# Gated cross-attention with FFN: small GpSimd steps moved to VectorE, x staged by tile, the second batch's context turned in 32x32 blocks, all orders rewritten

## The reference

```python
xn = layernorm(x)
scores = (xn @ ctx.T) / 16            # (B, 256, 1601), masked columns -> -1e30
attn = softmax(scores)
x = x + tanh(g_xattn) * where(any(mask), attn @ ctx, 0)
h = layernorm(x).as_e4m3()
gate = gelu(h @ wg0.as_e4m3()); ff1 = h @ wg1.as_e4m3()       # 256 -> 1024
x = x + tanh(g_ffn) * ((gate * ff1).as_e4m3() @ wlin.as_e4m3())
```

## Time and profile before

| | |
|---|---|
| median of 3 runs | 133.41 us |
| the profiled execution's own time | 132.98 us |
| its span, first to last instruction | 131.2 us |
| granted TensorE clock | full (1.00, the 2.4 GHz level) over the span |
| busy, TensorE / VectorE / ScalarE / GpSimd | 120.9 / 89.1 / 90.8 / 93.2 us |

### The profile page before, as it was taken

One profiled execution on the slowest core, in us unless ns is written; L12 is line 12 of the kernel. 1 busy time (PEld: TensorE's weight loads), 2 busy tenths in 40 slices (PEclk: granted clock), 3 DMA queues, 4 the chain that ended last, 5 costly groups with the idle time before them and its releaser, 6 DMA issues.

```text
span 131.2 us, 2509 instructions
## 1 busy us (share of the span) xinstructions
PE 120.9 (92%) x846; PEld 103.1 (79%) x846; DVE 89.1 (68%) x187; ACT 90.8 (69%) x141; POOL 93.2 (71%) x90
## 2 busy tenths in 40 slices
PE   6849999999799999899999899999999959999991
PEld 4438978989789998779999599999987955454780
DVE  1347479989996874998673984394694665767852
ACT  3189999699978893979665680599672876947300
POOL 3069930579999899999999999999989833930000
PEclk9999999999999999999999999999999999999999
DMA  1697999699992997503600069015000000000035
GB/s 44 195 383 229 397 233 261 105 179 188 296 254 102 182 179 126 179 1 85 235 5 0 12 180 308 5 12 148 0 0 7 2 0 0 0 0 5 0 124 196
DMA packets 33908, 15.93 MB, mean 121 GB/s; under 512 B 25700, under 2 KB 32616, under 8 KB 33896
## 3 DMA queue, kind: packets, MB, share of 16 engines
q1 hardware_dynamic: 33608, 15.77, 46.4%
q10 hardware_dynamic: 288, 0.00, 0.1%
HBM read 14.72 MB, written 1.05 MB: 120 GB/s over the span
## 4 chain that ended last, share of the span: by engine, by line
PE 37%; POOL 35%; ACT 8%; DVE 6%; issue 5%; DMA 5%; SPq 1%; POOLq 0%; DVEq 0%; ACTq 0%
POOL ws L436 7%; POOL cTl_a L430 7%; PE scores L774 7%; PE pv L750 6%; POOL wq L437 6%; POOL chl_a L422 5%; PE ring L790 5%; DMA xs<-in_x_dram 5%; PE ring L719 5%; PE pv L754 3%; PE scores L736 3%; PE scores L732 3%; PE scores L737 3%; POOL chl_b L422 2%; POOL cTl_b L430 2%
## 5 line engine op out<-in xcount | busy, mean ns | idle before, releaser
L481 ACT ACTIVATE pT_hi<-ring 128x512 fp32r<-128x512 f32 (+1 forms) x32 | 15.3, 508 | 8.7 <-PE pv L754 4.5
L422 POOL TENSOR_TENSOR chl_a<-cn,chl_a 128x1024 fp32r<-128x1024 f32 x8 | 19.2, 2399 | 1.9 <-ACT chl_a L496 1.9
L599 DVE TENSOR_TENSOR pT_lo<-ring,pT_hi 128x512 fp32r<-128x512 f32 (+1 forms) x32 | 17.8, 578 | 3.3 <-ACT pT_hi L481 3.3
L750 PE MATMUL pv<-chl_a,pT_hi 128*128 128x256 f32 x128 | 18.6, 287 | 0.1
L617 DVE CUSTOM_DVE_ANT_0 sp<-scores,bias 128x1024 f32<-128x1024 f32 (+1 forms) x16 | 15.6, 983 | 4.1 <-PE scores L737 1.9
L422 POOL TENSOR_TENSOR chl_b<-cn,chl_b 128x1024 fp32r<-128x1024 f32 (+1 forms) x8 | 12.5, 1569 | 7.3 <-ACT chl_b L496 6.8
L719 PE MATMUL ring<-ident,sp 128*128 128x128 f32 (+1 forms) x104 | 16.0, 273 | 1.2 <-DVE cTl_b L599 0.7
L750 PEld LDWEIGHTS pv<-chl_a,pT_hi 128*128 128x128 f32 x128 | 16.4, 189 | 0.6 <-DVE xs L636 0.3
L516 ACT ACTIVATE sp<-sp,nb,sc 128x1601 f32<-128x1601 f32 x8 | 13.8, 1724 | 3.5 <-DVE nb L624 3.5
L750 PE MATMUL pv<-chl_b,pT_hi 128*128 128x256 f32 (+1 forms) x80 | 12.8, 291 | 2.2 <-ACT pT_hi L481 1.3
L436 POOL TENSOR_TENSOR ws<-ws,wg 128x1024 f32<-128x1024 f32 x6 | 14.3, 2390 | 0.6 <-DVE wg L641 0.6
(11 more groups left out here) (80 smaller groups left out, 278.0 us busy)
## 6 DMA issues: line engine op xcount, KB each, us to landing
cn<-in_ctx_dram SPq DMA_DIRECT2D x12, 512.0 KB, 4.8
cb<-in_ctx_dram SPq DMA_DIRECT2D x16, 192.0 KB, 3.7
ws<-in_L_ffn_w_gating_dram SPq DMA_DIRECT2D x4, 512.0 KB, 5.4
ws<-in_L_ffn_w_linear_dram SPq DMA_DIRECT2D x2, 512.0 KB, 4.5
out_dram<-xs SPq DMA_DIRECT2D x8, 128.0 KB, 1.8
mrow<-in_mask_BxS_bk_dram SPq DMA_DIRECT2D x4, 200.1 KB, 6.0
xs<-in_x_dram SPq DMA_DIRECT2D x2, 256.0 KB, 5.4
xs<-in_x_dram SPq DMA_DIRECT2D x1, 512.0 KB, 5.1
```

Of the source, the lines that this page charges most:

```text
L422: nc.gpsimd.tensor_tensor(chl(b, g)[0:parts, :, D:2 * D], cn[0:parts, t0:t1, :], chl(b, g)[0:parts, :, 0:D].bitcast(f32), ALU.subtract).th ...
L481: nc.scalar.activation(dst, bank_view(f, size), ACT.Copy, scale=-1.0 if f[0] == "X" else 1.0).then_inc(hi_ready, 1)
L599: nc.vector.tensor_tensor(dst, bank_view(f, size), hi.bitcast(f32), ALU.subtract).then_inc(freed, 1)
L750: nc.tensor.matmul(pv[:, 0:D], pT_hi[0:parts, t, :], ctx[0:parts, t - t0, D * part:D * (part + 1)], start=(t == 0 and part == 0), stop=False)
```

## The change

- `BLOCKED` is now (1, 2, 3): batch 1's context is also loaded as 32x32 blocks (eight more transfers, step `b1`), turned on VectorE (`D1:0` to `D1:2`), its low parts written by GpSimd. Its six C steps are gone (`C1:6`, the tail, stays), and its mask bias takes the one-instruction form. The context of batch 1 as it stands is now loaded in the other row order.
- x is staged in five parts, `XPART`: tiles 0, 1, 2-3, 4-5, 6-7, in four transfers (128, 128, 256 and 512 KB). G, F, K and X go by these parts.
- The factor 1/16 of the scores goes into the turned x (`FOLD`) and no longer into the scale.
- `F` on GpSimd is left with the power and the negation, `Q` with the power and the bias, `v` is gone. VectorE adds eps itself in `stats` (a wait on its own aggregate, then one small instruction), and in `O` compares the maximum with -0.5e30 (`vl`) and multiplies with it and with tanh(g).
- All five order strings are rewritten.

```diff
-    BLOCKED = (2, 3)
+    BLOCKED = (1, 2, 3)
+    XPART = [(0, 1), (1, 2), (2, 4), (4, 6), (6, 8)]
+    FOLD = 1.0 / D ** 0.5
     SP_ORDER = steps("""
-        x0 c0:0 x1 c0:1 c0:3 c0:2 m1 m0 c1:0 x2 c1:1 w0 m2 c1:2 b2 c1:3 c2:0 w1 m3 c2:1 w2 b3 c2:3 w3 c3:1 c2:2
-        c3:3 c3:0 c3:2 w4 w5 o3 o0 o1 o4 o5 o6 o2 o7""")
+        c0:2 x0 c0:3 c0:1 x1 c0:0 x2 m0 b1 x3 m1 c1:3 w0 c1:0 c1:1 w1 b2 c1:2 c2:1 c2:0 w2 m2 m3 c2:3 b3 c3:1
+        c2:2 c3:0 c3:3 w3 c3:2 w4 w5 o3 o1 o2 o4 o5 o0 o6 o7""")
     ACT_ORDER = steps("""
-        K0 R0:0 C0:1 C0:0 X0 R0:1 C0:3 C0:2 R0:2 C0:5 C0:4 C0:6 B0 K1 C1:1 C1:0 X1 E0 W0 T0:0 C1:3 T0:1 R0:3
-        R1:0 C1:2 C1:4 R1:1 T0:2 J E1 T0:3 C1:5 B1 C1:6 D2:0 K2 T1:0 D2:1 W1 T1:2 T1:1 E2 ...
+        R0:2 C0:6 K0 R0:3 C0:5 X0 C0:2 C0:4 K1 J R0:1 C0:0 C0:1 X1 C0:3 B0 K2 R0:0 E0 T0:0 D1:0 T0:1 X2 D1:1
+        T0:2 W0 D1:2 C1:6 T0:3 E1 B1 K3 T1:1 T1:3 R1:1 T1:2 X3 T1:0 R1:0 W1 K4 E2 ...
...
     DVE_ORDER = steps("""
+        G0 C0:6 C0:5 X0 G1 C0:2 C0:4 G2 C0:0 C0:1 C0:3 X1 M0:0 M0:1 M1:0 D1:0 T0:0 O0 D1:1 T0:1 X2 D1:2 M1:1 W0
+        T0:2 T0:3 C1:6 G3 A0 M2:0 T1:3 T1:1 G4 O1 X3 T1:0 ...
...
     POOL_ORDER = steps("""
-        F0 Z0:0 Z0:1 F1 Z0:2 Z0:3 Z1:0 Z1:1 v0 I0 F2 D2:0 v1 D2:1 F3 v2 Q0 I1 Z1:3 Z1:2 D2:2 Z2:1 v3 I2 D3:1 Q1
-        D3:0 Z2:0 Z2:3 Z2:2 Q2 D3:2 v4 Q3 I3 v5 Z3:0 v6 Q4 Z3:1 Z3:3 Z3:2 I4 Q5 Q6 v7 Q7 I5""")
+        F0 Z0:3 F1 Z0:2 F2 Z0:1 Z0:0 D1:0 D1:1 D1:2 I0 Z1:1 Z1:0 I1 D2:0 Z1:3 D2:1 Z1:2 F3 D2:2 Z2:1 Z2:0 I2
+        D3:0 Z2:3 D3:1 Z2:2 D3:2 Q0 Q1 F4 Q2 Q3 I3 Z3:0 Z3:1 Z3:2 Z3:3 I4 Q4 Q5 Q6 Q7 I5""")
     PE_ORDER = steps("""
+        C0:6 C0:5 C0:4 X0 C0:2 C0:0 C0:3 C0:1 X1 S0:0 S0:1 S0:2 S0:3 S1:0 S1:1 T0:0 X2 T0:1 S1:2 V0:0 T0:2 S1:3
+        V0:1 T0:3 C1:6 S2:0 S2:1 V0:2 T1:3 V0:3 T1:1 ...
...
+        ... V5:3 H0 V6:0 H1 T7:0 T6:2 V6:1 V6:2 V6:3 T7:3 T7:1 H2 T7:2 V7:0 V7:1 V7:2 V7:3 N2 H3 H4 ...
...
-                link(nc.gpsimd.tensor_scalar(ve[:, a:z], mv[:, a:z, 1], EPS, float(D), ALU.add, ALU.mult))
-                link(nc.gpsimd.tensor_tensor(sc[:, a:z], ve[:, a:z], half_pow[:, 0:QT], ALU.pow))
-                nc.gpsimd.tensor_scalar(lim[:, a:z], sc[:, a:z], 0.5 * NEG, 1.0, ALU.mult, ALU.mult)
+                link(nc.gpsimd.tensor_tensor(sc[:, a:z], ve[:, a:z], half_pow[:, 0:z - a], ALU.pow))
                 nc.gpsimd.tensor_scalar(nsc[:, a:z], sc[:, a:z], -1.0, 1.0, ALU.mult, ALU.mult).then_inc(sc_ready, 1)
...
-                nc.gpsimd.tensor_scalar(vt[:, j:j + 1], nb[:, j:j + 1], lim[:, j:j + 1], tg[:, 0:1],
-                                        ALU.is_lt, ALU.mult).then_inc(vt_ready, 1)
...
-                link(nc.gpsimd.tensor_scalar(ve2[:, j:j + 1], mv2[:, j, 1:2], EPS, 1.0, ALU.add, ALU.mult))
...
+                last.then_inc(mean, 1)
+                dve.wait_ge(mean, count)
+                nc.vector.tensor_scalar(eps_[:, tiles[0]:tiles[-1] + 1], mv_[:, tiles[0]:tiles[-1] + 1, 1], EPS, None,
+                                        ALU.add).then_inc(var, 1)
...
             def factor(j):
+                link(nc.vector.tensor_scalar(vl[:, j:j + 1], mx[:, j, 0:1], mx[:, j, 1:2], -0.5 * NEG,
+                                             ALU.max, ALU.is_gt))
+                if j == 0:
+                    dve.wait_ge(tg_ready, 1)
                 dve.wait_ge(exp_ready, act_e[("E", j)])
                 link(nc.vector.reciprocal(ri[:, j:j + 1], rs[:, j:j + 1]))
-                dve.wait_ge(vt_ready, pool_v[("v", j)])
-                nc.vector.tensor_scalar(fo[:, j:j + 1], ri[:, j:j + 1], vt[:, j:j + 1], None, ALU.mult).then_inc(fo_ready, 1)
+                nc.vector.tensor_scalar(fo[:, j:j + 1], ri[:, j:j + 1], vl[:, j:j + 1], tg[:, 0:1],
+                                        ALU.mult, ALU.mult).then_inc(fo_ready, 1)
```

More of the change, by code:

```diff
@@ L204, in pair @@
             return (hbanks[i], None) if i < 2 else (hbanks[(i - 2) % 3], None if i == 4 else i - 2 if i < 4 else i - 3)
-        x_in = [sem(f"x_in{i}") for i in range(3)]
+        x_in = [sem(f"x_in{i}") for i in range(4)]
         g_in = sem("g_in")
@@ L581, in link, with stats @@
                 dve.wait_ge(dve_link, links[0])
-            def stats(tiles, st_, mv_, ready):
+            def stats(tiles, st_, mv_, mean, count, eps_, var):
                 for j in tiles:
@@ L692, in fill @@
                     pe.wait_ge(xc_ready, act_k[("K", f[1])])
-                    todo = [(bank[:, (KD * q + k) * P:(KD * q + k + 1) * P], xc[:, QT * f[1] + q, k * P:(k + 1) * P], P)
-                            for q in range(QT) for k in range(KD)]
+                    j0, j1 = XPART[f[1]]
+                    todo = [(bank[:, (KD * i + k) * P:(KD * i + k + 1) * P], xc[:, j0 + i, k * P:(k + 1) * P], P)
+                            for i in range(j1 - j0) for k in range(KD)]
                 elif f[0] == "N":
```

101 lines of the change are left out of this document (47 added, 54 removed).

## The result

The changed kernel takes 133.96 us (median of 20 runs, 132.61 to 134.97) beside 132.95 us for the kernel before in the same runs (median of 20, 132.38 to 133.53). The ratio is 1.0055, 95% interval 1.0028 to 1.0082: slower by half a per cent, where 129.8 us with a range of 127.0 to 133.0 was predicted. The profiled execution took 134.40 us with a span of 132.4, against 132.98 and 131.2.

The account below looks back on a forecast made before the run. TensorE's sum of work was taken as the bound, with GpSimd just in time beside it. 132.98 - 2.6 - 1.0 gave 129.4 us, or 129.8 at the median's level; range 127.0 to 133.0.

Parts of the forecast that it names:

- first part of the path: Start up to T1: ScalarE limits, scores can start at 13.0, first exponential at 19.0, T1 at 31.4 us.
- the sum: Whole kernel: 132.98 - 2.6 - 1.0 = 129.4 us for an execution like the profiled one, 129.8 at the median's level.
- TensorE's work: Six batch 1 context pieces of four transposes go, 0.44 us each, 2.6 us less; all other steps stay.
- GpSimd's work: 8.1 us added, 7.0 removed, net 1.1 or less; first D step at 24.1, 71 us to the last Z.
- VectorE's work: Low parts out, block transposes, vl and eps additions (5 us) in; sum +4.7 us, covered by the matmuls.
- When things arrive: Load landings: x0 at 7.0, tail c0:3 at 7.3, b1 at 20.6 to 21.2 us; TensorE begins at 7.3.
- E0: First exponential, on ScalarE behind the first tile's scores: predicted to start at 19.0 us, against 19.42 before.
- rival 2: b1 lands late: every microsecond D1:0 starts past 21.8 counts fully; 131.0 to 133.1 us, chance 0.18.
- First term: Path up to T1: T1 starts at 31.4 instead of 34.04 us, -2.6 us, all of the removed transposes.
- The rest: Behind T1: same work, TensorE sets the end; 1.0 of the 1.32 us wait at 106.72 goes, -1.0 us.
- rival 4: VectorE's thirteen eps additions wait for GpSimd's long instructions, 12 us more on VectorE; 135.8 us if half counts; chance 0.14.

Follow-up runs that it names:

- e10: Changed kernel with C0:4 read out before C0:2, TensorE kept busy by idle matmuls, and two-element eps additions done as two of one element: 130.45 us.
- e12: Kernel before with only eps and the bound comparison moved to VectorE, one-element eps additions, and TensorE kept busy by idle matmuls: 130.10 us.
- e15: e8 with its eps additions done one element at a time: 130.10 us.
- e17: Changed kernel with 24 score matmuls of 512 columns done as two of 256, so as many matmuls as before: 132.73 us.
- e18: e17 with 33 opening matmuls and idle ones in TensorE's early pauses, orders and additions as in the changed kernel: 131.08 us.
- e8: Changed kernel with 33 opening matmuls, idle ones in early pauses, C0:4 read out before C0:2, and G2 moved later on VectorE: 130.05 us.
- small steps alone: Kernel before with only eps and the bound comparison moved to VectorE, its orders unchanged but for the v steps: 133.27 us.
- e11: Kernel before with 30 opening matmuls instead of 22 and nine idle ones behind X0's transposes: 132.97 us.

## Why the prediction was wrong

The step that failed is the first part of the path. It took ScalarE's list for the limit, put TensorE's pauses, its clock and its ring banks at nothing, and so had T1 at 31.4 us, 2.6 earlier than before. Measured was 37.10, 3.1 later. Second, the sum took what lies behind the last matmul as fixed; it grew by 1.1 us.

The distance from the forecast divides into three steps of runs: 133.96 - 132.73 = 1.2 us for the code packet between the stores (1.65 by the ratios), 132.73 - 131.08 = 1.65 for the granted clock, 131.08 - 130.05 = 1.0 for the readout order and G2's place, taken together (0.6 of it is the form of G2's addition, by e10). What is left, 130.05, is 0.25 above the forecast, and that is luck: there T1 gained 0.2 us and not 2.6, and the stretch from T1 to the last product 3.0 and not 1.0.

- **TensorE's work**: right. The six pieces are gone, nothing came for them. What they gave was used up ahead of T1 even with all mended (e12 and e15).
- **GpSimd's work**: right in its sum (71.4 us from the first D to the last Z, 71 predicted), wrong in its start (29.5 instead of 24.1), which hangs on the first part.
- **VectorE's work**: right. Thirteen additions and eight vl took 2.3 + 1.6 = 3.9 us, where I had 5, and they are covered.
- **When things arrive**: x0 at 7.21 (7.0) and b1, its last transfer by 20.8 (20.6 to 21.2), were right. The tail c0:3, the third transfer and the first thing that TensorE transposes, came late, and TensorE began at 8.20 instead of 7.3.
- **The first part of the path** failed. "S0:0 can start at 13.0", "E0 at 19.0"; measured 17.52 and 24.39. The estimate took ScalarE's list for the limit, since it had been busy 12.97 of 13.4 us in the earlier trace rows. It is busy 9.19 now; it waits. Of the 5.4 us, the runs give the clock 2.3 (e17 to e18), the readout order with G2's place 1.0 (e18 to e8), and the trace gives the late tail 0.9. The remaining 1.2 is not separated. The price that rival 2 gave was borne out: T1 is 5.7 us later than predicted, D1:0 5.3. I never asked what the new order of loads does to TensorE's idle time ahead of its first data: a pause of 1.75 us stood there in the earlier trace rows without loss of clock in that execution, here it was 2.29. Nor did I follow the ring banks through the new strings, where the swapped pair C0:4, C0:2 can be seen.
- **First term** (T1 at 31.4, -2.6 us): +3.1 us, as a consequence.
- **The rest** (-1.0 us): right in sign and too small, -2.9 us from T1 to the last product (85.2 against 88.1 us). I had named the 1.32 us wait of the earlier trace rows alone. It is gone, and so are nearly all others. The small steps alone give this (88.4 to 85.3 us, e11 to e12), so it needs none of the new orders.
- **The sum** took what lies behind the last matmul as fixed. It grew by 1.1 us.
- **Rivals.** None of them was what happened. The result is on the side of rival 4, but not by its mechanism: the thirteen additions cost 2.3 us in all. Its mechanism is real where the operand has two elements, which I had noted as a difference without drawing the line there; in the small steps alone it costs about 2 us. (I counted nine additions of one element; there are ten, and three of two.) The wait of rival 2 didn't occur: the first D step had its data.

What stays open: how the packet of code holds up the stores (its share of the DMA engines in that window is 3.5%; whether the stores wait for its place in a queue isn't shown), and what sets its place beside the count of matmuls. The spread of the changed kernel's executions (2.4 us) doesn't come from it: with the packet moved it is 2.5 us still (e17), with TensorE kept busy as well 0.17 (e18).

## What to carry to other kernels

Read a new order of first steps for TensorE's pauses, not only for its work: one that pauses for 2 us before its first data and again for a bank can lose two more through its clock, and 47 idle matmuls in the pauses bought most of them back (-1.65 us here, and a spread of 0.17 us instead of 2.5). When a small operation moves to VectorE beside a busy GpSimd, give it one element per partition; two one-element additions (0.21 us) are cheaper than one of two elements (up to 2.24). Work taken off the critical engine early is worth nothing if the start of the path gets longer by as much. And compare where the last product starts before comparing totals: a change in instruction count can move the end by a microsecond with no work behind it, and a run that adds instructions to test something else moves it too.
